# Attention and expert layer on one core: where TensorE's maxima products stand among the expert pieces

## The reference

```python
x = x + attention(layernorm(x), ctx, ctx)     # softmax(q k^T / sqrt(32)) v, per head
x = x + moe(layernorm(x), router_w, w1, w2)

def moe(x):
    vals, idx = top_k(x @ router_w.T, 2)      # two experts per token
    weights = softmax(vals)
    gate, up = split(rows_of(e) @ w1[e].T)    # 704 channels each
    y[e] = (silu(gate) * up) @ w2[e].T
    return sum over the two experts of weights * y
```

## Time and profile before

| | us |
|---|---|
| median of 3 runs | 10138.48 (10130.77 to 10140.67) |
| profiled execution, its own time | 10143.92 |
| its span, first to last instruction | 10142.2 |
| TensorE busy | 9157.7 (90% of the span) |
| VectorE busy | 5165.7 (51%) |
| ScalarE busy | 3662.6 (36%) |
| GpSimd busy | 2411.2 (24%) |

### The profile page before, as it was taken

The page is one execution under the profiler, slowest core; times in us unless marked ns, Lnnn a source line. Parts: engine busy times, 40 slices in busy tenths (PEclk is TensorE's granted clock), DMA queues, the critical chain, the costliest instruction groups (busy, mean ns, idle before and its releaser), DMA issues. The chain is left out here.

```text
span 10142.2 us, 169689 instructions
## 1 busy us (share of the span) xinstructions
PE 9157.7 (90%) x55016; PEld 4601.1 (45%) x55016; DVE 5165.7 (51%) x10907; ACT 3662.6 (36%) x5426; POOL 2411.2 (24%) x3894
## 2 busy tenths in 40 slices
PE   4466689999999999999999999999999999989989
PEld 3322234444444444444444444444444444444457
DVE  7766665555555555555555555555555554222212
ACT  3444444333333333443333433333443343200001
POOL 0022222222222222222222222222222222211111
PEclk8688889999999999999999999999999999999999
DMA  9742134444444444444444444444444444454444
GB/s 364 298 186 75 53 104 127 134 134 130 122 130 123 134 133 131 128 132 119 131 134 130 120 133 121 132 134 131 127 133 119 131 136 128 122 189 145 160 167 165
DMA packets 455196, 1431.29 MB, mean 141 GB/s; under 512 B 90088, under 2 KB 110568, under 8 KB 454128
## 3 DMA queue, kind: packets, MB, share of 16 engines
q1 hardware_dynamic: 360240, 1132.12, 33.2%
q0 software_dynamic: 94016, 287.65, 12.2%
HBM read 1034.41 MB, written 408.21 MB: 142 GB/s over the span
## 5 line engine op out<-in xcount | busy, mean ns | idle before, releaser
L866 PE MATMUL e_y<-e_xt,e_w 128*128 128x512 f16 x14520 | 3518.6, 380 | 0.0
L950 ACT ACTIVATE a_p<-a_sc,a_escale 128x512 f32<-128x512 f32 x2048 | 1406.3, 687 | 3621.2 <-PE a_sc L696 3555.8
L1342 DVE TENSOR_REDUCE a_nmax<-a_mx 128x2 f32<-128x512 f32 x2048 | 1411.6, 689 | 1897.6 <-PE a_mx L713 1882.6
L866 PEld LDWEIGHTS e_y<-e_xt,e_w 128*128 128x128 f16 x14520 | 1372.6, 98 | 1597.5 <-issue 244.4
L887 PE MATMUL e_y<-e_w,e_yt 128*128 128x512 f16 x7480 | 1857.7, 380 | 0.0
L713 PE MATMUL a_mx<-a_ks,a_qs 96*128 96x256 f16 x4096 | 816.9, 282 | 564.0 <-DVE a_nmax L1342 559.2
L682 PE MATMUL a_pv<-a_p,a_v 128*64 128x512 f32 x4096 | 1104.1, 664 | 0.0
L1156 POOL TENSOR_TENSOR a_xres<-a_att,a_xres 128x128 f32<-128x128 f32 x1024 | 469.3, 479 | 2424.9 <-DVE a_att L1367 1886.5
L887 PEld LDWEIGHTS e_y<-e_w,e_yt 128*128 128x128 f16 x7480 | 691.0, 98 | 767.6 <-issue 127.4
L713 PEld LDWEIGHTS a_mx<-a_ks,a_qs 96*128 96x128 f16 x4096 | 370.0, 99 | 1078.2 <-DVE a_nmax L1342 684.9
L696 PE MATMUL a_sc<-a_qs,a_ks 128*128 128x512 f16 x2048 | 794.8, 388 | 58.0 <-ACT a_p L950 45.7
(11 more groups left out here) (231 smaller groups left out, 9787.7 us busy)
## 6 DMA issues: line engine op xcount, KB each, us to landing
e_w<-w_parts SPq DMA_DIRECT2D x935, 512.0 KB, 3.6
f_w<-w_parts SPq DMA_DIRECT2D x153, 512.0 KB, 4.9
w_parts<-w_parts SPq DMA_DIRECT2D x136, 512.0 KB, 4.9
h_w<-w_parts SPq DMA_DIRECT2D x136, 512.0 KB, 6.0
a_x<-in_x SPq DMA_DIRECT2D x64, 1024.0 KB, 5.8
a_xres<-in_x SPq DMA_DIRECT2D x64, 1024.0 KB, 7.8
out<-a_xres SPq DMA_DIRECT2D x64, 1024.0 KB, 8.6
xn_parts<-a_xhl SPq DMA_DIRECT2D x64, 1024.0 KB, 9.6
```

The source lines that it names most:

```text
L866: last = pe.matmul(Y[:, bank, :], w1r[:, t % RING, h, pw, :], xT[:, px, h, :], start=r == 0, stop=r == 3 * HT - 1)
L950: act.activation(PT[:, kv % 2, h, tt, :], SC[:, :], ACT.Exp, scale=escale[:, sp_:sp_ + 1]).then_inc(n["exps"], 1)
L1342: dve.reduce_max(nmax[:, half, kv * G + 2 * gp:kv * G + 2 * gp + 2], MX[:, :, :], AX.X, negate=True).then_inc(n["maxed"], 1)
```

## The change

In every eighth the first expert piece of a quarter moves behind the maxima of that quarter, and behind what follows them (O, V, the transposes of the maxima, the counts). TensorE's order becomes S T M O E0 E1, S M V E2 E3, S T M E4 E5, S T M E6 E7. Only TensorE's order changes; no instruction is added or left out, and the streams of the other engines are the same, instruction by instruction.

```diff
                 for k in range(8):
                     score(i, k, par, 0)
                     turn_q(i, k, par, fused)
-                    experts(i, 8 * k, par, fused)
                     max_score(i, k, par, 0)
                     turn_o(i, k)
+                    experts(i, 8 * k, par, fused)
                     experts(i, 8 * k + 1, par, fused)
                     score(i, k, par, 1)
-                    experts(i, 8 * k + 2, par, fused)
                     max_score(i, k, par, 1)
                     values(i, k, par)
+                    experts(i, 8 * k + 2, par, fused)
                     experts(i, 8 * k + 3, par, fused)
                     score(i, k, par, 2)
                     turn_k(i, k, fused)
                     if k in (2, 4):
                         router(i, k // 2 - 1)
-                    experts(i, 8 * k + 4, par, fused)
                     max_score(i, k, par, 2)
                     turn_max(i, k)
+                    experts(i, 8 * k + 4, par, fused)
                     experts(i, 8 * k + 5, par, fused)
                     score(i, k, par, 3)
                     turn_x(i, k, fused)
-                    experts(i, 8 * k + 6, par, fused)
                     max_score(i, k, par, 3)
                     if k == 6:
                         count(i)
+                    experts(i, 8 * k + 6, par, fused)
                     experts(i, 8 * k + 7, par, fused)
```

## The result

The changed kernel takes 10222.01 us (median of 4 runs, 10213.34 to 10230.62), the kernel before beside it 10139.58 (4 runs, 10130.77 to 10145.11): a ratio of 1.0082, 95% interval 1.0065 to 1.01. That is 82 us slower, where 112 were forecast. The profiled execution of the changed kernel has a span of 10211.6 us, 69.4 more than that of before.

What follows compares the result with a forecast made beforehand. TensorE, 90% busy, bounds the kernel, plus M's waits for reduction R. Terms 1.30 + 0.27 + 0.55 + 0.30 - 0.20 = 2.2 us, times 51 iterations = 112 us, give 10250 us; 8-in-10 range 10185 to 10325.

Steps and rivals of the forecast that it cites:

- The four terms of new waits: Added TensorE waits per iteration at M(eighth, quarter): M(0,3) +1.30, M(1,1) +0.27, M(2,1) +0.55, M(4,1) +0.30 us.
- The head: M(0,1) at an iteration's start: largest wait stays, except a shorter DVE instruction wait in even iterations, -0.2 us per iteration.
- the bounds 0 and 1.15 per even iteration: Possible us saved at M(0,1) from DVE's 4.20 us instruction wait, against about 3.05 without expert weights loading; 0.4 taken.
- the prediction's own signs: Timeline checks: M(0,3) waits about 1.8 us; M(0,1) stays near 1.3 and 8.4; shrinking by microseconds would prove it wrong.
- The close places: M(3,2), M(4,0), M(5,0), M(5,2), M(5,3), M(6,1): 0.1 to 0.4 us left, costed nothing; rival (16%): they wait, 10311 us.
- M(6,1): Maxima in eighth 6, behind the copies of T: a close place with 0.1 to 0.4 us left, costed at nothing.
- The sum: New waits less the head's gain: 2.2 us per iteration, times 51 iterations, 112 us slower.
- The prediction's 51 iterations: Iterations 13 to 63, where attention's maxima run in full with the expert blocks; the multiplier of 2.2 us.
- The clock: Rival (9%): the wait at M(0,3) lowers TensorE's granted clock, about 1.7 us more each iteration, 10337 us.
- Fewer interruptions: Rival (7%): expert run broken 32 instead of 64 times per iteration, saving 4.5 us against 2.2 lost, 10021 us.
- DVE catching up at the head: Rival (9%): shorter wait at M(0,1) takes back the new waits in eighths 0 to 4; time stays near 10138 us.
- The total of waits: Sign: TensorE's wait for R in 2000 to 8000 us rises by about 95, to some 360 us.

Runs made afterwards that it cites:

- E2: Not a run: a piece of expert matmuls on TensorE, first of an eighth's second quarter; the change moves it behind that quarter's maxima and V.
- E7: Not a run: the last piece of expert matmuls in an eighth on TensorE; the load of the second weights waits for this product.

## Why the prediction was right, and where not

**Which measure counts, and the direction:** right. What decided was the slack of each M from the event that releases DVE, less one piece of 1.30 us. The four terms of new waits came within 0.06 us each (table), 2.44 measured for 2.42 forecast. That they add up without later places taking them back is shown by putting one and five of the pieces back.

**The head, the mis-sized term:** the prediction had -0.20 us per iteration, measured were -1.54. Three things in that step were off. The mechanism itself was right: E7 and the loads behind it came 1.30 us later against DVE. But of the bounds 0 and 1.15 per even iteration I took 0.4, and the first wait gave the whole (4.21 to 3.04 us, -1.17). The bounds were made from this wait alone, and the second one, at L1326, stood in the earlier trace rows with 3.03 us and was left out: on average over the 22 heads it fell from 3.44 to 1.57, -1.87. Together -3.04 per even iteration, nearly the whole -3.09 of the stall there. By one of the prediction's own signs this step was wrong: M(0,1) was not to shrink by microseconds, and in even iterations it did. I called those 1.15 all that could come back at the head; the later loads alone, with nothing moved on TensorE, give the same 3.53 at the head as the change. A wait for instructions that is shorter in one part of the program than in another is a price with a cause, and both such waits of the chain belonged in the bound.

**The close places, held but for one:** M(3,2), M(4,0), M(5,0), M(5,2) and M(5,3) kept slacks of 0.24, 0.18, 0.16, 0.95 and 1.87 us on average (to the end of R; 0.06 of it is used by every M), as the sums had it or better. One of them in the changed kernel, R(3,1) and M(3,2):

```profile
5373.73 0.68 DVE L1342 TENSOR_REDUCE a_nmax<-a_mx 128x2 f32<-128x512 f32 x1
...
5374.65 0.38 PE L713 MATMUL a_mx<-a_ks,a_qs 96*128 96x256 f16 x2
```

M(6,1) was missed, +0.30. I counted every piece as six matmuls. E2 of eighth 6 holds eight transposes of gathered rows as well (line 787), as the timeline of before shows from T to M(6,1):

```profile
5100.63 0.62 PE L735 MATMUL a_tr<-ident,a_qsrc 128*128 128x128 f16 x8
...
5104.11 0.69 DVE L1342 TENSOR_REDUCE a_nmax<-a_mx 128x2 f32<-128x512 f32 x1
...
5104.56 0.81 PE L887 MATMUL e_y<-e_w,e_yt 128*128 128x512 f16 x3
5105.20 0.61 PE L787 MATMUL a_tr<-ident,e_xg 128*128 128x128 f16 x8
5105.65 0.81 PE L887 MATMUL e_y<-e_w,e_yt 128*128 128x512 f16 x3
5106.30 0.38 PE L713 MATMUL a_mx<-a_ks,a_qs 96*128 96x256 f16 x2
```

R(6,0) ends 5104.80 - 5100.63 = 4.17 us after T in both kernels. The piece is worth 5106.30 - 5104.56 = 1.74, not 1.30, so the slack of 5106.30 - 5104.80 - 0.06 = 1.44 went to -0.30.

**The sum:** 2.22 - 1.34 (head) + 0.30 (M(6,1)) and 0.14 in small terms make the 1.32 measured. With the head as measured and all else as forecast it would have been 0.88, 51 x 0.88 = 45 us or some 10183, just below the range: that the time lies inside it is in part luck, since M(6,1), put at nothing, stood against the head, and since the medians lie 13 us further apart than the profiled spans. The prediction's 51 iterations are 52, because the maxima run in full in iteration 64 too (M(0,3) sits idle for 1.62 us at 8524.07 us in the changed kernel); that is 2 us of the forecast.

**The rivals.** *The clock* did not fall there: 1.00 around the wait of 1.78 at M(0,3), and in 2000 to 8000 us both traces have the lower level (1.2 GHz) only near the heads of even iterations, 22 times each. At the head of the even iteration above, where TensorE waits 6.24 us, the two matmuls of M behind it take 0.61 us instead of 0.39, and the granted clock is 0.82 over 5167 to 5186 us; the kernel before has that too (0.75 over 5134 to 5153 us, and the 0.61 in the earlier trace rows). The Trainium skill, "TensorE: Matmul & The Clock Gate", section "Why this matters for your kernels", tells of idle gaps that bring back the half clock; the trace agrees at the long wait, and the short one shows that not every gap does. *Fewer interruptions* paid nothing: 32 breaks of the expert run less per iteration, and the time without stalls is 128.72 us for 128.66, so nothing was saved. What the Trainium skill says in "TensorEngine Tiling (Array Packing)", section "Key Properties", of a drain at a change of tiling mode shows no price here at M, which works on 96 of the rows between matmuls on 128; whether that is a change of mode no run here shows. *The close places* became one wait, not six. *DVE catching up at the head* was the rival that held a part of the truth: 1.5 us of the 2.7 that the other places lost came back there, but through the loads and the waits behind the branch, not through DVE's work.

**The total of waits:** TensorE's wait for R was to rise from 267 to some 360 and is listed with 281.7. Of the 78 that are missing, 1.34 x 43 = 58 are the head; the rest is that the listed idle time leaves out about 0.16 us of each wait, and that the new waits of about 0.3 at M(1,1), M(4,1) and M(6,1) are for the most part too short to be listed at all. The stalls worked out from starts rose by 1.26 x 43 = 54.

## What to carry to other kernels

Where an engine that works in order releases another, count the slack of each wait from the event that lets the slow side start, in pieces with all that each piece holds, and move only the places that have the slack: five of these 32 moves cost all that the change lost, 26 gained nothing together, and one gained, through the loads that it shifted. Read every wait for instructions behind a loop's branch on the chain that ends last, and look at which large transfers start at that moment; here 1.30 us of shift was enough, and the runs with the loads later show no price for it.

## What was not expected of the hardware

VectorE's waits behind the branch are longer when large loads start just before it. With six loads of 512 KB issued 0.32 us ahead of the last instruction before the branch, the two waits take 4.21 and 3.44 us on average; with the same loads issued 0.98 us behind it, 3.04 and 1.57; with none on the way, 2.98 and 1.35. The page of the profile lists instructions as DMA queues of their own; here are the queues around the head, in the kernel before (5134 to 5146 us; packets, MB, share of 16 engines):

```profile
q1 hardware_dynamic: 848, 3.10, 77.2%
q0 software_dynamic: 144, 0.07, 5.7%
q14 instruction: 6, 0.05, 1.9%
```

and in the one with only the loads later (5070 to 5082 us):

```profile
q0 software_dynamic: 164, 0.15, 19.3%
q14 instruction: 8, 0.07, 5.5%
```

Instructions and weights are thus moved at the same moment. The instruction packets' own time is not longer beside the loads (1.9% for 6 packets, 5.5% for 8), which speaks for a delay ahead of their transfer. That is argued, not shown: these traces do not tell where the time goes, nor what sets the 3 us and the 1.4 us that stay when no weights are loaded.

One operation of VectorE takes over twice as long beside one of GpSimd's. The low half (L1493, from f32 to f16) of eighth 4 is shown before, with the GpSimd operation that runs beside it, and then after, where that operation has ended when it starts:

```profile
5073.45 2.13 POOL L1161 TENSOR_TENSOR a_xhl<-a_xres,a_xhl 128x1024 f16<-128x1024 f32 x1
5074.30 1.84 DVE L1493 TENSOR_TENSOR e_yt<-e_th,e_yt 128x512 f16<-128x512 f32 x1 [0.16 <-ACT e_yt L1036]
...
5390.45 0.69 DVE L1493 TENSOR_TENSOR e_yt<-e_th,e_yt 128x512 f16<-128x512 f32 x1
```

Over 44 iterations it takes 1.88 us there before and 0.69 after; in eighth 5, where it ran beside L1166 before, 1.72 and 0.78. In all, L1493 is busy for 306.0 us before and 198.3 after, 108 of the 140 us by which VectorE's busy time fell: the same instructions did not take the same time. No M waits for these two in either kernel, so no term of the sum moves, and no run varies this by itself.
